# Attention of a four-block kernel: query halves as the outer loop, double steps of two key tiles, value products a double step late in one bank, a half's maxima by one matmul and two DMAs

## What is computed

```python
e1 = _conv1x1(x, w1, b1, a1).reshape(N, -1, HW)   # 32 channels, PReLU
e2 = _conv1x1(x, w2, b2, a2).reshape(N, -1, HW)
asm = _conv1x1(x, wa, ba, aa).reshape(N, C, HW)   # 64 channels, PReLU
score = jnp.einsum('nci,ncj->nij', e1, e2)
score = jax.nn.softmax(score, axis=2)
out = jnp.einsum('nij,ncj->nci', score, asm)
```

## Time and profile before

| what | us |
|---|---|
| three timed runs | 695.98, 698.48, 700.29; median 698.48 |
| span of the profiled execution | 697.9 |
| VectorE, ScalarE, GpSimd busy in it | 535.1, 429.5, 385.2 |

### The profile page before, as it was taken

How to read it: one execution, slowest core, us unless ns; L and a number is a source line. 1 busy time by engine, 2 the same in 40 slices (tenths; PEclk the granted TensorE clock), 3 DMA queues, 4 the chain that set the end, 5 groups by cost and what they waited for, 6 DMA issues and landing times.

```text
span 697.9 us, 8622 instructions
## 1 busy us (share of the span) xinstructions
PE 625.1 (90%) x2812; PEld 275.6 (39%) x2812; DVE 535.1 (77%) x857; ACT 429.5 (62%) x737; POOL 385.2 (55%) x243
## 2 busy tenths in 40 slices
PE   3795888888789989999989999999999999986996
PEld 1232332233353332234434444343444444335982
DVE  6996899999934465888858787887878888685547
ACT  2478689899644331235555765748476565787772
POOL 2454788887512140216939779595968979430000
PEclk9997999999999997999989999999999999998999
DMA  9000000000015482404003040300304020200006
GB/s 328 7 0 0 1 0 0 0 0 0 1 45 140 112 199 54 106 1 91 0 1 90 1 91 0 71 21 9 83 0 91 0 31 1 30 1 0 1 1 241
DMA packets 28533, 32.36 MB, mean 46 GB/s; under 512 B 16976, under 2 KB 17104, under 8 KB 28368
## 3 DMA queue, kind: packets, MB, share of 16 engines
q1 hardware_dynamic: 27056, 27.33, 15.3%
q10 hardware_dynamic: 1440, 4.55, 2.7%
HBM read 5.83 MB, written 4.19 MB: 14 GB/s over the span
## 4 chain that ended last, share of the span: by engine, by line
PE 58%; DVE 19%; issue 8%; ACT 7%; POOL 4%; DMA 1%; SPq 1%; DVEq 0%; POOLq 0%; ACTq 0%
PE PS L1723 15%; PE PS L1710 10%; PE PS L1688 9%; PE PS L1599 5%; DVE RB L476 3%; PE PS L1608 2%; PE PS L1677 2%; PE PS L1743 2%; DVE RB L552 2%; DVE PS L544 2%; DVE RB L851 2%; DVE RB L559 1%; PE PS L1850 1%; DVE SM L456 1%; DVE SM L692 1%
## 5 line engine op out<-in xcount | busy, mean ns | idle before, releaser
L692 DVE TENSOR_REDUCE SM<-PS 128x1 f32<-128x512 f32 x256 | 165.0, 683 | 65.3 <-PE PS L1688 64.7
L1154 ACT ACTIVATE RB<-PS 128x512 f32<-128x512 f32 x256 | 138.9, 594 | 88.0 <-PE PS L1710 86.9
L1391 POOL TENSOR_TENSOR RB<-RB 128x1024 f32<-128x1024 f32 x60 | 141.1, 2372 | 7.1 <-DVE RB L721 4.8
L1710 PE MATMUL PS<-R 98*128 98x512 f32 x256 | 95.5, 452 | 1.3 <-ACT RB L1154 1.3
L1688 PE MATMUL PS<-R 96*128 96x512 f32 x256 | 88.7, 418 | 6.9 <-DMA R<-R 3.2
L1723 PE MATMUL PS<-RB 128*64 128x512 f32 x320 | 85.4, 616 | 0.0
L1710 PEld LDWEIGHTS PS<-R 98*128 98x128 f32 x256 | 38.8, 189 | 83.4 <-ACT RB L1154 53.9
L1526 PE MATMUL PS<-RA,W 128*128 (+1 forms) x128 | 63.1, 636 | 8.7 <-DVE RB L552 5.3
L1688 PEld LDWEIGHTS PS<-R 96*128 96x128 f32 x256 | 48.7, 193 | 43.1 <-DVE SM L692 18.9
L1391 POOL TENSOR_TENSOR EX<-EX,RB 128x1024 f32<-128x1024 f32 x24 | 56.5, 2373 | 0.8
L1723 PE MATMUL PS<-RB,RA 128*64 128x512 f32 x192 | 52.7, 627 | 0.0
(11 more groups left out here) (186 smaller groups left out, 1111.7 us busy)
## 6 DMA issues: line engine op xcount, KB each, us to landing
R<-WS SPq DMA_DIRECT2D x72, 128.0 KB, 2.4
X<-x SPq DMA_DIRECT2D x8, 512.0 KB, 7.4
...
```

Of the source, the lines that this page charges most:

```text
L692: v.tensor_reduce(MX[:, par, tile, h:h + 1], bank(2 + h), AX.X, ALU.max)\
L1154: act(slot[:, h * HALF:(h + 1) * HALF], bank(4 + h), ACT.Exp).then_inc(s["p_ready"], 1)
L1391: i = g.tensor_tensor(out, out, PT[j % SLOTS][par], ALU.add)
L1710: mm(bank(4 + h), stack(b, par, 1)[0:98, j * P:(j + 1) * P], stack(b, par, 0)[0:98, h * HALF:(h + 1) * HALF]).then_inc(s["t_mm"], 1)
```

## The change

What it does, by engine:

- **Order of the scores.** The query half is now the outer loop, key tiles the inner one, and both images are done in each step: step n is half n // 8, key tile n % 8, with bank 4 for the first image and 5 for the second. A double step d holds steps 2d and 2d+1: four scores and four row products in the order S R S R R S R S, then whatever else is due, then two calls of value products, those of steps 2d-2 and 2d-1 (for d = 0, the last two of the pair before).
- **Value products** are accumulated in bank 0 alone, one query half after the other; bank 1 joins banks 2 and 3 for the row products of pairs 2 to 7. Row products go by tile, image, key half.
- **Maxima.** For a query half, one matmul makes 16 rows of 128 columns in bank 4; ScalarE copies them into a small tile `MT`, and SyncE moves them into the stacks with two DMAs. Sixteen matmuls and four copies of 512 columns a pair become two and two, with four DMAs. These stand on SyncE's queue between the pair's eight high moves and its four low ones.
- **Values.** PReLU is now relu(-y) on ScalarE (`negative`) and one pass on VectorE (`value`), in place of two passes on VectorE.
- **Sums** are made for each half; the exponentials lie in eight slots of 1024 columns. GpSimd adds half 0's, then makes the low part of pair p+2, for pair 0 then the normalized input of pair 3, then adds half 1's.
- **End.** VectorE's adds for the last pair are spread over it, with the scaling of the half before between them; ScalarE takes half 0's reciprocal after its four normalizations.

The diff, cut to what these points and the prediction speak of:

```diff
+        PT = [RB[:, j * L:(j + 1) * L] for j in range(CHUNKS)]
+        SA = [RB[:, (8 + k) * L:(9 + k) * L] for k in range(4)]
...
-        STEPS = [(0, 0), (1, 0), (0, 1), (1, 1)] + [(j, par) for j in range(2, CHUNKS) for par in range(2)]
+        CBANK, SBANK, MBANK = [6, 7], [7, 6], 4
+
+        def rows_bank(q, r):
+
+            if q < 2:
+                return 2 + r % 2
+            return 1 + (32 * (q - 2) + r) % 3
...
+            def maxima(q, h):
+
+                sp.wait_ge(s["m_copied"], 2 * q + h + 1)
+                for par in range(2):
+                    rows = stack(q % 3, par, 0)[96:98, h * HALF:(h + 1) * HALF].bitcast(F32)
+                    sp.dma_start(rows, MT[8 * par:8 * par + 8, :])\
+                        .then_inc(s["m_in"], 16)
...
-            stacked(1, 1)
-            stacked(2, 2)
-            for q in range(3, PAIRS):
-                stacked(q, q % 3)
+            stacked(1, 1, False)
+            stacked(1, 1, True)
+            maxima(0, 0)
+            for p in range(PAIRS):
+                maxima(p, 1)
+                if p + 2 < PAIRS:
+                    stacked(p + 2, (p + 2) % 3, False)
+                if p + 1 < PAIRS:
+                    maxima(p + 1, 0)
+                if p + 2 < PAIRS:
+                    stacked(p + 2, (p + 2) % 3, True)
...
+            def value(q, c):
+
+                v.wait_ge(s["v_neg"], 2 * q + c + 1)
+                chunks = V[q % 3][:, c * 4:c * 4 + 4, :].rearrange("p c m -> p (c m)")
+                v.scalar_tensor_tensor(chunks, chunks, OMAA, bank(CBANK[c]), ALU.mult, ALU.add)\
                     .then_inc(s["v_done"], 1)
...
+            def attend(p, lag=True, extra={}):
+
+                for d in range(CHUNKS):
+                    if d == 0:
+                        both_parts(p, 1)
+                    if d == 1:
+                        add_first(p, 0)
+                    if d in (2, 6):
+                        biased(p + 1, d // 6)
+                    if d in (3, 7):
+                        value(p + 1, d // 7)
+                    if d in (4, 5) and p + 2 < PAIRS:
+                        operands(p + 2, d - 4)
+                    if d == 4:
+                        both_parts(p + 1, 0)
+                    if d == 5:
+                        add_first(p, 1)
+                    for m in range(4):
+                        maximum(p + 1, 4 * d + m)
+                    if d in extra:
+                        extra[d]()
+                    if lag and d == 0:
+                        scaled(p - 1, 0)
+                        residual(p - 1, 0)
+                    if lag and d == 1:
+                        end_stats(p - 1, 0)
+                    if p > 1 and d == 2:
+                        end_stats(p - 2, 1)
+                    if lag and d == 7:
+                        scaled(p - 1, 1)
+                        residual(p - 1, 1)
...
+            def add(h, j):
+
+                v.wait_ge(s["p_ready"], 32 * (PAIRS - 1) + 16 * h + 2 * j + 2)
+                out = SA[(2 * (PAIRS - 1) + h) % 4]
+                v.tensor_tensor(out, out, PT[j], ALU.add).then_inc(s["add_dve"], 1)
...
+            q = PAIRS - 1
+            both_parts(q, 1)
+            link(end_stats(q - 2, 1))
+            coefs_stat(0, q - 1)
+            coefs_var(GN3A, 0, q - 1, 6)
+            scaled(q - 1, 0)
+            residual(q - 1, 0)
+            add_first(q, 0)
+            v.wait_ge(s["first_added"], 2 * q + 1)
+            end_stats(q - 1, 0)
+            add(0, 2)
+            coefs_shift(GN3A, 0, q - 1)
...
+            for j in range(3, CHUNKS):
+                add(0, j)
+            scaled(q - 1, 1)
+            residual(q - 1, 1)
+            add_first(q, 1)
+            v.wait_ge(s["first_added"], 2 * q + 2)
+            add(1, 2)
+            add(1, 3)
+            end_stats(q - 1, 1)
+            add(1, 4)
+            add(1, 5)
+            scaled(q, 0)
+            residual(q, 0)
+            add(1, 6)
             end_stats(q, 0)
-            end_stats(q, 1)
-            add(3)
-            add(4)
-            for j in (5, 6, 7):
-                add(j)
-            q = PAIRS - 1
-            for h in range(2):
-                scaled(q, h)
-                residual(q, h)
-                i = end_stats(q, h)
-            link(i)
+            add(1, 7)
+            scaled(q, 1)
+            residual(q, 1)
+            link(end_stats(q, 1))
...
+            def negative(q, c):
+
+                a.wait_ge(s["asm_done"], 2 * q + c + 1)
+                chunks = V[q % 3][:, c * 4:c * 4 + 4, :].rearrange("p c m -> p (c m)")
+                act(chunks, bank(CBANK[c]), ACT.Relu, scale=-1.0).then_inc(s["v_neg"], 1)
...
+            def attend(p, lead=True, lag=True, extra={}):
+
+                for d in range(CHUNKS):
+                    probs(p, 2 * d)
+                    if d == 1 and lag:
+                        product_out(p - 1, 1)
+                    if d == 5:
+                        product_out(p, 0)
+                    probs(p, 2 * d + 1)
+                    z = p + 2 < PAIRS
+                    if d == 0 and lag:
+                        inverse(p - 1, 0)
+                    if d == 1:
+                        maxima(p, 1)
+                    if d == 5 and lead:
+                        maxima(p + 1, 0)
+                    if d in (2, 6) and lead:
+                        negative(p + 1, d // 6)
+                    if d in (3, 4) and z:
+                        linear_part(p + 2, d - 3)
+                        relu_part(p + 2, d - 3)
+                    if d == 5 and z:
                         high_z(p + 2, 0)
                         high_z(p + 2, 1)
-                    if n in (6, 7) and lag:
-                        inverse(p - 1, n - 6)
-
+                    if d == (7 if lead else 5) and lag:
+                        inverse(p - 1, 1)
+                    if d in extra:
+                        extra[d]()
+
...
-            attend(PAIRS - 1, 1, lead=False, extra=late)
+            attend(PAIRS - 1, lead=False, extra={1: lambda: root(GN3A, 0, PAIRS - 2), 5: lambda: hats(2),
+                                                 7: lambda: hats(3)})
...
-            for h in range(2):
-                product_out(PAIRS - 1, h)
-            for h in range(2):
-                inverse(PAIRS - 1, h)
+            inverse(PAIRS - 1, 0)
+            product_out(PAIRS - 1, 1)
+            inverse(PAIRS - 1, 1)
...
+            def sums(p, h):
+
+                g.wait_ge(s["first_added"], 2 * p + h + 1)
+                out = SA[(2 * p + h) % 4]
                 for j in range(2, CHUNKS):
+                    g.wait_ge(s["p_ready"], 32 * p + 16 * h + 2 * j + 2)
+                    g.tensor_tensor(out, out, PT[j], ALU.add).then_inc(s["add_done"], 1)
...
+                if q < 2:
+                    need(t, s["s_read"], 32 * q + r - 1)
+                else:
+                    t.wait_ge(s["s_read"], max(64, 32 * q + r - 2))
+                mm(bank(rows_bank(q, r)), stack(b, par, 0)[0:96, tile * P:(tile + 1) * P],
+                   stack(b, par, 1)[0:96, jh * HALF:(jh + 1) * HALF]).then_inc(s["s_mm"], 1)
...
+            def max_rows(q, h):
+
+                if q or h:
+                    t.wait_ge(s["p_ready"], 32 * (q if h else q - 1) + (7 if h else 23))
+                else:
+                    t.wait_ge(s["zf_done"], 4)
+                t.wait_ge(s["m_ready"], 2 * q + h + 1)
+                mm(PS[0:16, MBANK if q or h else 7, 0:P], MB[:, h].rearrange("p a k t -> p (a k t)"), IB[:, :])\
+                    .then_inc(s["mrow_mm"], 1)
+
+            def scores(p, b, n, par):
+
+                h, j = divmod(n, CHUNKS)
+                if j == 0 and par == 0:
+                    t.wait_ge(s["m_in"], 32 * (2 * p + h + 1))
+                need(t, s["p_ready"], 32 * p + 2 * n + par - 1)
+                if n in (4, 12) and par == 0 and not (n == 12 and p == PAIRS - 1):
+                    t.wait_ge(s["m_copied"], 2 * p + 2 + n // 12)
+                mm(bank(4 + par), stack(b, par, 1)[0:98, j * P:(j + 1) * P],
+                   stack(b, par, 0)[0:98, h * HALF:(h + 1) * HALF]).then_inc(s["t_mm"], 1)
...
+                    need(t, s["acc_read"], 2 * p + h)
...
-                    i = mm(PS[par * C:(par + 1) * C, h, :], V[b][:, j, par * C:(par + 1) * C],
-                           PT[j % SLOTS][par][:, h * HALF:(h + 1) * HALF],
-                           start=(j == 0), stop=(j == CHUNKS - 1))
+                    i = mm(PS[par * C:(par + 1) * C, 0, :], V[b][:, j, par * C:(par + 1) * C],
+                           PT[j][:, par * HALF:(par + 1) * HALF], start=(j == 0), stop=(j == CHUNKS - 1))
...
+                for d in range(CHUNKS):
+                    scores(p, b, 2 * d, 0)
                     if lead:
-                        if n == 2 and p + 2 < PAIRS:
-                            operands_free(p + 2)
-                        rows(p + 1, (b + 1) % 3, n, 0)
```

(32 more changed lines are left out.)

490 lines of the change are left out of this document (186 added, 304 removed).

## The result

| | before | after |
|---|---|---|
| median of four runs, us | 698.5 (696.0 to 700.3) | 724.4 (723.2 to 728.6) |
| span of the profiled execution | 697.9 | 721.7 |
| mean granted clock in it | 0.972 | 0.954 |

The ratio is 1.039, with a 95% interval of 1.034 to 1.044: slower, as forecast, but above the range, whose upper end was 720. The forecast of 705.2 us is 19 us short.

The account below looks back on a forecast made before the run. It took TensorE alone to set the pace in attention. The terms -0.5 + 3.8 - 6.5 + 0 + 3.9 + 5.0 + 1.0 = +6.7 took the span from 697.9 to 704.6 us, the median to 705.2; range 691 to 720.

Parts of the forecast that it names:

- TensorE's work, 36.4 us a pair: Inner pair: TensorE's work falls from 40.13 us, 2.8 less by grouping and 0.9 less by the maxima.
- The rival that grouping saves nothing: Alternating scores and rows saves nothing: TensorE's work 39.2, a pair 41.3, total 714 us; chance 0.14.
- Waits of an inner pair, 3.7 us: TensorE waits 1.8 for VectorE in double step 1, 1.5 for stacks at pair start, 0.4 in double step 5.
- the rule of the Trainium skill: SyncE's stack moves: a DMA's fixed cost is mostly its receipt; wait 0.2 instead of 1.5, sum 6.5 us lower.
- Pairs 2 to 6, no change: Inner pairs: 36.4 us of work plus 3.7 of waits make 40.1 us, as before.
- Pair 0, +3.8: First pair: work 35.0, 5.0 of waits from two row-product banks, 2.8 for VectorE: 42.8 instead of 39.0 us.
- Pair 1, -6.5: Second pair: GpSimd wait and half-clock stretch gone, 38.9 instead of 45.4 us.
- The old stall: Pair 1 before: a wait of 2.33 us for GpSimd's third operand, with a stretch at clock 0.50, forecast to go.
- Pair 7, +3.9: Last pair, to its last exponential: two waits of 1.6 us for ScalarE's bank copy and 0.7 of smaller ones.
- The end, +5.0: Behind the last exponential: last reciprocal 13.8 us later instead of 8.8; TensorE idles nearly 9 us.
- Start and rest: Ahead of the first score: 0.5 us less; after attention: 1.0 more for half clock, transposes and third block otherwise unchanged.
- The clock falls at the waits: Rival: clock falls in most of pairs 0 to 6, about 3 us each, total 720 us; chance 0.12.

Follow-up runs that it names:

- e3: The changed kernel with VectorE's first sums behind the four maxima and ScalarE's copies of high parts (with SyncE's moves) earlier: 700.2 us.
- e8: e5 with bank 1 for the last pair's first-half products and, in pair 0, three banks for row products from the third double step: 682.2 us.
- e1: The changed kernel with the first sum of each half moved behind the four maxima of its double step on VectorE: 707.0 us.
- e2: The changed kernel with ScalarE's two copies of high parts, and with them the moves on SyncE, at an earlier place: 718.4 us.
- e4: The kernel before the change, with GpSimd's normalized input of pair 3 made two sums earlier in pair 0: 693.9 us.
- e5: e3 with the end of attention reordered on VectorE and ScalarE, VectorE's last two sums ahead of scaling the first half: 694.3 us.

## Why the prediction was wrong

The direction and the places of the waits were right, and the size was not. Point by point, against the span of 704.6 that the sum gave (measured 721.7, 17.1 more):

- **TensorE's work, 36.4 us a pair: mis-sized by 1.5.** It is 37.9 (TensorE's busy time in a pair of e3 and e8). Value products came as forecast, 1.87 us a double step. Alternating scores and rows takes 2.18 instead of 2.1, and the first double step of a pair is longer still (4.4 us in e8); the mean is about 4.1 instead of 3.95 (an estimate, 37.9 less the rest of a pair's work as the prediction had it). Grouping and maxima together save 2.2 us a pair, not 3.7. The rival that grouping saves nothing, with 39.2, was as close (1.3 off).
- **Waits of an inner pair, 3.7 us: right in place, 0.6 too long.** 1.81 and 1.1 to 2.2 were read, 0.2 in double step 5; the undisturbed pairs give 41.05 - 37.9 = 3.1. e1 and e2 remove them one at a time and show that they are VectorE's first sum and SyncE's queue. On the second, the rule of the Trainium skill (DMA: Bandwidth & Descriptors, Anatomy of one DMA), given for GpSimd's path, puts most of a DMA's fixed cost into its receipt; by it the wait would have been 0.2 us. Here SyncE's queue spends 5.13 us on eight issues, and starting them 3.8 us earlier removes the wait: the row on the queue decided rightly.
- **Pairs 2 to 6, no change: 8.0 more.** The clock in pairs 3, 4 and 6 makes 5.0 of it; more work, less what the waits were shorter, makes 3.0.
- **Pair 0, +3.8: +8.7.** The waits for VectorE are there (eight, 6.4 us, where 7.8 were forecast); 3.3 us are clock. The rest is TensorE's work, some 38 us (38.2 busy in e3's pair 0, at full clock) where the sum had 35.0. e8 shows that having two banks instead of three cost 3.1 us.
- **Pair 1, -6.5: -3.2.** The old stall is gone, and e4 shows it to be worth 5.3 alone. A wait of 2.81 for VectorE, larger than the usual 1.8, 1.7 us of clock and 1.2 more of work take its place.
- **Pair 7, +3.9: +7.1.** Two waits of 1.60 as forecast, and 3.3 us of clock. Without the clock 33.5 us, where the forecast had 33.6.
- **The end, +5.0: +5.6.** The last reciprocal comes 14.5 us after the last exponential (forecast 13.8); VectorE idles 5.35 us (forecast 6), TensorE 8.63 (forecast 9). e5 takes it back.
- **Start and rest.** The start gave 1.3 instead of 0.5, and the transposes and the third block did not pay the 1.0 of clock; together 2.9 less.

**The step that failed** is the one that kept the clock out of the sum: inside attention it was put at nothing. The prediction had it as a rival, "The clock falls at the waits", at 720 and a chance of 0.12, on the grounds that the wait of 1.85 us in the earlier trace rows went without a fall and the one of 2.33 in the earlier trace rows did not. The profiled execution lost 13.3 us to the clock in pairs 0 to 7, of the 17.1 that the span is over the sum; the rival's 15 were nearly it, though a fall costs 1.7 us and not 3. Its own condition, falls in most of pairs 0 to 6, is met in five of seven. New waits were the core of the forecast: up to the last exponential the trace of after has fourteen of 1.1 us and more in attention, that of before one, and seven of the fourteen have a stretch at half clock behind them. A rival that rests on the forecast's own waits should have had a share of the sum. Pair 7, whose two waits were forecast too and which lost 3.3 us, was not among its places. The Trainium skill (TensorE: Matmul & The Clock Gate, HAM oscillation — how this bites in real kernels) describes a kernel that returns to half rate at each wait for a DMA between bursts. The trace of after agrees in pairs 3 and 6, behind waits of 2.02 and 2.24 us; at the waits for a DMA of 1.11 to 1.14 us in pairs 2, 4 and 5 it doesn't happen. The second failure, smaller and partly hidden by the shorter waits, is the size of TensorE's work: 37.9 us a pair instead of 36.4.

**Where the expected gain went.** The regrouping saves 2.2 us of TensorE's work in an inner pair, as e3 and e8 show. In the change, each inner pair gives back 3.1 in two waits, which moving the first sums on VectorE and the copies of high parts on ScalarE removes but for 0.5 to 0.7, and the clock takes 10 us more than before (13.3 against 3.6).
